# Block 1's causal mask on GpSimd, V projections from fp16 halves, another order of stages

## The chip, the cores and the metric

One Trainium2 chip, one core of it. The metric is device time in microseconds (us) of one execution. The kernel before took 839.89 us, the median of 3 runs (839.71 to 840.85).

## The reference, cut to what matters

The input x is (8, 256, 256): 8 batches of 256 tokens with 256 channels. Two blocks follow one another, each a residual sum over one LayerNorm:

```python
xn = _layernorm(x)
x = x + attn0(xn) + ffn0(xn)      # block 0
xn = _layernorm(x)
x = x + attn1(xn) + ffn1(xn)      # block 1
```

- attn0 and attn1 have 16 heads of 16 channels and a causal mask. attn0 adds ALiBi slopes, and clamps the probabilities from below at 1e-10, so a masked entry still counts. attn1 is a plain causal softmax: a masked entry is zero.
- ffn0 is a mixture of 8 experts (silu(x Wg) * (x Wu)) Wd, weighted per token by a router. ffn1 has ternary weights (256 to 1024 to 256) and a GELU between them; its output is quantized to 4 bits by a scale over the whole tensor, so no output can be written before the last batch's ffn1 is known.

## The kernel before, in words

Each batch is a set of tiles of 128 partitions; tokens are 2 tiles (NT), channels 2 (NK). The five engines each run their own list of steps, and the code of a step on an engine is a branch `if name == ...` in that engine's `do`. Orders are written out by hand in `FIRST_ORDER` (batch 0 of block 0, and the weights' preparation), `STEADY_ORDER` (a loop of 6 iterations: block 0 of batch n together with block 1 of batch n-1, and the beginning of batch n+1, marked +), `LAST_ORDER` and `FINAL_ORDER`. A number is a head of attention 0 (score, norm, turn, value steps at lags 0, 1, 3, 4). TensorE and the DMA queue of SyncE take this order as it is; ScalarE and VectorE shift steps by the offsets in `LAG`; GpSimd takes it as it is. Instructions of one engine are executed in order, and semaphores make them wait for other engines.

Steps that matter here:
- **ln0a, ln0b, tr0** (ln1a, ln1b, tr1 for block 1): VectorE computes the statistics and normalizes in place; GpSimd adds the output bias into `xb` (L790) and takes the power for rstd (L792); TensorE transposes in fp32 (L1032). ScalarE copies the result twice, to `xt` in fp32 (L902) and to `xt_hi` in fp16 (L903), and VectorE subtracts to get `xt_lo` (L1314). `xe_hi` and `xe_lo` are GpSimd's copies for the experts.
- **q, k, gate, up, down, w1**: products of fp16 halves, three products (hi*hi, lo*hi, hi*lo), or two where the weight is exact. Weights were multiplied by `WSCALE` = 16 before they were split (step **split**: ScalarE hi, VectorE or GpSimd lo).
- **v0:0, v0:1, v1** (L1070): the V projection, in fp32 from `xt` and `wv_sb`; v0 has the router's 8 columns beside the 256.
- **b, mp, m**: row maxima of block 1's scores, brought to a row `max_row` by way of `pieces` (GpSimd) and a bf16 product.
- **s:0 to s:7** (two heads each, `turn_ps[0]` and `[1]`): transposed scores on TensorE, plus the negated maximum (L1174), plus the mask: a product of `ident_b` with `later_b`, which holds -1e30 over the diagonal (L1177). ScalarE takes the exponential of 128x384 into `et` (L990).
- **y:0 to y:3** (four heads each): products of `et` with V (L1202) and with `ones` (L1208), the sum of the exponentials; VectorE divides (L1494, L1496). Then **op1** (L1126), the output projection.
- **up** on GpSimd: the low half `h0_lo` (L820) of the hidden layer, which **down** needs.
- **setup:1** on GpSimd builds `bias0`, slopes times distance (L801) plus the mask in `bias1` (L804), for block 0's scores.

In the loop GpSimd does nothing else than `pieces`, `xb`, rstd, `xe`, `h0_lo` and the low halves of h1.

## Time and profile before

| | us |
|---|---|
| median of 3 runs | 839.89 |
| profiled execution | 839.0 |
| its span | 837.3 |
| TensorE (PE) busy | 695.7 (83%) |
| VectorE (DVE) busy | 578.1 (69%) |
| ScalarE (ACT) busy | 478.3 (57%) |
| GpSimd (POOL) busy | 228.6 (27%) |

The profile comes from one execution. Rows name engine, line of the kernel, instruction, output and inputs, and shape. TensorE's matmuls are pipelined: the distance from one start to the next is what one costs, and the duration shown is longer than that. A number in brackets is the time in which the engine was idle before the row, with the instruction that ended the wait.

### The profile page before, as it was taken

To read this page: it belongs to the slowest core of one execution; us is meant where nothing else is said; L and a number is where in the kernel's file an instruction comes from. 1 tells how busy PE (TensorE), PEld (TensorE's weight loads), DVE (VectorE), ACT (ScalarE), POOL (GpSimd) and SP (SyncE) were. 2 spreads that over 40 slices of the span, in tenths; PEclk is the share of its full clock that TensorE was granted. 3 is DMA by queue.
4 is the path that set the end of the run, shared out by engine and by line. 5 is a ranking of instruction groups with operands and counts; after the bars stand their busy time and mean duration, and the time that the engine had idled before them with its cause. 6 is when DMAs were issued, how large, how long until landed. Compare 5 with 4: busy or idle time off the path is not lost.

```text
span 837.3 us, 19783 instructions
## 1 busy us (share of the span) xinstructions
PE 695.7 (83%) x6519; PEld 502.6 (60%) x6519; DVE 578.1 (69%) x2197; ACT 478.3 (57%) x1237; POOL 228.6 (27%) x260
## 2 busy tenths in 40 slices
...
GB/s 199 243 107 114 1 51 64 89 15 27 114 0 101 13 101 29 94 10 57 83 14 87 13 100 26 97 4 32 107 0 101 13 100 14 101 2 14 118 203 71
DMA packets 49544, 57.10 MB, mean 68 GB/s; under 512 B 5056, under 2 KB 40000, under 8 KB 49472
## 3 DMA queue, kind: packets, MB, share of 16 engines
...
## 4 chain that ended last, share of the span: by engine, by line
PE 61%; DVE 14%; ACT 8%; issue 8%; DMA 5%; ACTq 1%; SPq 1%; POOL 1%; DVEq 1%; POOLq 0%
PE gen_ps L1084 15%; PE gen_ps L1095 8%; PE value_ps L1202 7%; PE gen_ps L1058 5%; PE gen_ps L1126 3%; PE gen_ps L1070 3%; DVE probs L1461 3%; PE gen_ps L1115 3%; PE value_ps L1208 3%; PE turn_ps L1177 2%; PE score_ps L1139 2%; ACT hid L950 2%; PE turn_ps L1168 2%; DMA gu_lo<-x_dram 1%; PE turn_ps L1149 1%
## 5 line engine op out<-in xcount | busy, mean ns | idle before, releaser
L962 ACT ACTIVATE probs<-probs,nmax 128x256 f32<-128x256 f32 (+1 forms) x256 | 113.4, 445 | 57.8 <-DVE nmax L1461 57.3
L820 POOL TENSOR_TENSOR h_lo<-hid,h_hi 128x512 f16<-128x512 f32 x64 | 76.6, 1197 | 204.8 <-ACT h_hi L943 204.8
L1084 PE MATMUL gen_ps<-xe_hi,gu_hi 128*128 128x256 f16 x512 | 103.3, 285 | 8.4 <-DVE gated L1407 4.3
L1461 DVE CUSTOM_DVE_ANT_0 probs<-score_ps,bias 128x256 f32<-128x256 f32 (+1 forms) x256 | 80.5, 352 | 35.4 <-PE score_ps L1141 24.6
L1084 PE MATMUL gen_ps<-xe_lo,gu_hi 128*128 128x256 f16 x512 | 102.2, 283 | 0.0
L1475 DVE CUSTOM_DVE_ANT_0 junk<-score_ps,bias 128x256 bf16<-128x256 f32 (+1 forms) x256 | 76.1, 354 | 37.3 <-PE score_ps L1141 33.3
L1084 PE MATMUL gen_ps<-xe_hi,gu_lo 128*128 128x256 f16 x512 | 101.8, 282 | 0.0
L990 ACT ACTIVATE et<-turn_ps 128x384 f32<-128x384 f32 x128 | 55.8, 488 | 69.0 <-PE turn_ps L1177 69.0
L1486 DVE TENSOR_SCALAR probs<-probs,rsum 128x256 f32<-128x256 f32 (+1 forms) x256 | 81.3, 360 | 4.6
L1139 PE MATMUL score_ps<-k_stack,q_stack 64*128 64x256 f16 x256 | 37.7, 291 | 46.0 <-DVE nmax L1461 36.2
L971 ACT ACTIVATE pt<-turn_ps 128x384 f32<-128x384 f32 x128 | 61.2, 480 | 23.4 <-PE turn_ps L1151 23.4
L1412 DVE SCALAR_TENSOR_TENSOR hid<-gated,gen_ps 128x512 f32<-128x512 f32 x64 | 43.8, 685 | 41.9 <-PE gen_ps L1084 39.7
L1423 DVE SCALAR_TENSOR_TENSOR acc<-gen_ps,w,acc 128x256 f32<-128x256 f32 x112 | 48.7, 476 | 23.5 <-PE gen_ps L1095 23.5
L1084 PEld LDWEIGHTS gen_ps<-xe_hi,gu_hi 128*128 128x128 f16 x512 | 49.4, 102 | 24.5 <-issue 17.7
L1139 PEld LDWEIGHTS score_ps<-k_stack,q_stack 64*128 64x128 f16 x256 | 12.4, 93 | 80.0 <-DVE nmax L1461 40.2
L939 ACT ACTIVATE tanh_sb<-gen_ps 128x512 f32<-128x512 f32 x64 | 37.9, 592 | 38.6 <-PE gen_ps L1084 38.2
L833 POOL TENSOR_TENSOR h_parts<-hid,h_parts 128x512 f16<-128x512 f32 x32 | 36.7, 1160 | 84.6 <-ACT h_parts L957 84.6
L1084 PEld LDWEIGHTS gen_ps<-xe_lo,gu_hi 128*128 128x128 f16 x512 | 52.1, 102 | 8.0
L943 ACT ACTIVATE h_hi<-hid 128x512 f16<-128x512 f32 x64 | 40.0, 625 | 29.2 <-DVE hid L1412 25.3
L1084 PEld LDWEIGHTS gen_ps<-xe_hi,gu_lo 128*128 128x128 f16 x512 | 51.8, 101 | 7.7
L1407 DVE SCALAR_TENSOR_TENSOR gated<-tanh_sb,gen_ps 128x512 f32<-128x512 f32 x64 | 43.8, 685 | 17.7 <-ACT tanh_sb L939 16.9
L1095 PE MATMUL gen_ps<-wd_hi,h_hi 128*128 128x256 f16 x256 | 49.8, 277 | 4.9 <-issue 4.6
...
## 6 DMA issues: line engine op xcount, KB each, us to landing
...
```

What stands on the lines that cost most here:

```text
L820: pool.tensor_tensor(h0_lo[:, e], hid0[:, e], h0_hi[:, e], ALU.subtract).then_inc(s_h0l, 1)
L962: last = act.activation(probs[:, k, lo:hi], probs[:, k, lo:hi], ACT.Exp, scale=-1.0, bias=nmax[:, k, j:j + 1], accum_out=esum[:, k, j:j + 1])
L971: act.activation(pt[:, slot:slot + 3].rearrange("p t q -> p (t q)"), turn_ps[s % 2][:, 0:3 * P], ACT.Copy).then_inc(s_ev[0], 1)
L990: act.activation(et[:, s % TURNED], turn_ps[hp][:, 0:3 * P], ACT.Exp).then_inc(s_ev[1], 1)
L1084: last = pe.matmul(g[:, S * f:S * f + S], w[:, st.arg, m, k, cols], xx[:, k, :], start=(i == 0), stop=(i == len(terms) - 1))
L1095: last = pe.matmul(g[:, D * t:D * t + D], h[:, st.arg % 2, f, P * t:P * t + P], w[:, st.arg, f, :], start=(i == 0), stop=(i == len(terms) ...
L1139: pe.matmul(score_ps[hp][:, 0:S], q[rows[hp], i, P:S], k[rows[hp], i, :], start=True, stop=True)
L1202: last = pe.matmul(value_ps[PAD * j:PAD * j + PAD, lo:S], v, seen, start=(t == 0 and r == 0), stop=(t == 1 and r == 1), skip_group_check=( ...
L1423: dve.scalar_tensor_tensor(acc[:, t], g[:, D * t:D * t + D], w8[:, t, e:e + 1], (xb[0] if st.place == 0 else acc)[:, t], ALU.mult, ALU.add)\
L1461: last = dve.tensor_tensor_reduce(out=probs[:, k, lo:hi], in0=g[:, lo:hi], in1=bias0[:, s, blo:S], scale=-1.0, scalar=BIG, op0=ALU.add, op ...
L1475: last = dve.tensor_tensor_reduce(out=junk[:, hp, lo:hi], in0=score_ps[hp][:, lo:hi], in1=bias1[:, blo:S], scale=-1.0, scalar=BIG, op0=ALU ...
L1486: last = dve.tensor_scalar(probs[:, k, lo:hi], probs[:, k, lo:hi], rsum[:, k, j:j + 1], CLAMP, ALU.mult, ALU.max)
```

## The change

- The mask of block 1 goes from TensorE to GpSimd: the matmuls on `later_b` are gone; after each exponential an `affine_select` on GpSimd puts 0 into the entries above the diagonal of `et`; y waits for it (new semaphore `s_mk`).
- V is computed from fp16 halves of x and of Wv with the scale of 16, three products instead of one in fp32. `xt` and its copy are gone. A step `vsplit` splits Wv. The scale is taken out by `ones` = 16 in block 1, by the copy of `at[0]` in block 0, by `half_t` for the router; the bias is multiplied by 16.
- The mask in `bias0` becomes a selection instead of an addition.
- In the first batch LayerNorm writes to `acc` instead of over `x0`, so that it does not wait for the additions of the bias, which come behind the start of the weight loads.
- The four orders and the offsets of ScalarE and VectorE are others, and GpSimd has offsets too.

```diff
...
+       "gpsimd": {"s": 1, "up": 1, "s:6": -2, "last.b:1": 3, "v0:1": 1, "b:4": 4, "last.up": 2,
...
-    setup:0 ln0a split:1 xe split:0 ln0b split:3 tr0 setup:2 split:2 v0:0 q0 l0 k0 setup:1 split:5 rt1 gate:0 v0:1
...
+    ln0a setup:0 ln0b split:0 split:3 tr0 setup:2 xe split:2 vsplit:0 split:1 v0:0 q0 k0 gate:0 setup:1 l0 split:5 rt1
+    v0:1 split:4 up:0 gate:1 0 rt2 split:7 1 up:1 split:6 down:0 2 gate:2 3 down:1 4 up:2 split:8 gate:3 5 split:9
...
-    0 ln1a 1 ln1b gate:0 up:0 rt1 2 tr1 3 rt2 q1 k1 4 down:0 5 gate:1 6 up:1 7 gate:2 v1 w1:3 w1:0 w1:1 w1:2 l1 8 h1:0
-    up:2 9 10 h1:1 down:1 11 h1:2 gate:3 b:1 h1:3 up:3 down:2 12 13 14 15 b:0 16 gate:4 b:3 17 mp:0 up:4 b:4 18 down:3
-    b:2 +ln0a mp:1 w2 b:5 m:0 19 s:1 gate:5 op0 +ln0b s:0 b:6 +tr0 gate:6 up:5 down:4 s:2 +q0 b:7 y:0 s:3 +k0 up:6 +l0
-    +xe y:1 m:1 down:5 s:4 gate:7 +v0:0 s:5 up:7 s:6 y:2 s:7 down:7 y:3 +v0:1 down:6 op1
+    0 1 ln1a gate:0 2 ln1b up:0 rt1 tr1 3 rt2 4 q1 k1 5 gate:1 down:0 6 up:1 gate:2 w1:3 w1:0 l1 w1:2 w1:1 v1 7 8 h1:0
+    up:2 9 gate:3 10 h1:1 down:1 11 h1:2 b:1 h1:3 up:3 12 down:2 13 14 down:3 15 b:0 16 gate:4 17 b:3 mp:0 up:4 +ln0a
+    mp:1 18 b:2 w2 b:4 19 m:0 gate:5 s:1 b:5 down:4 +ln0b op0 s:0 b:6 +tr0 up:5 b:7 s:2 gate:6 +q0 +k0 s:3 y:0 +l0
+    up:6 m:1 gate:7 s:4 y:1 s:5 up:7 down:5 s:6 y:2 s:7 +v0:0 down:6 y:3 down:7 +v0:1 op1 +xe
...
-        wv_sb = [sb("wv0_sb", [P, NK, D + E]), sb("wv1_sb", [P, NK, D])]
+        wv_hi = [sb("wv0_hi", [P, NK, D + E], F16), sb("wv1_hi", [P, NK, D], F16)]
+        wv_lo = [sb("wv0_lo", [P, NK, D + E], F16), sb("wv1_lo", [P, NK, D], F16)]
...
-        later_b = sb("later_b", [P, NT, P], BF16)
...
-        xt = sb("xt", [P, NK, S])
...
+        et_flat = et[:].rearrange("p s q -> p (s q)")
+        wv_raw = [et_flat[:, 0:NK * (D + E)], et_flat[:, NK * (D + E):NK * (2 * D + E)]]
...
+                if n.reg is None and n.off == 1:
+                    sp.wait_ge(s_xb[0], NT)
...
-                pool.memset(ones[:, C:2 * C], 1.0).then_inc(s_tab, 1)
+                pool.memset(ones[:, C:2 * C], WSCALE).then_inc(s_tab, 1)
-                pool.affine_select(out=later_b[:], in_=later_b[:], compare_op=ALU.is_ge, fill=MASKED, base=0,
-                                   pattern=[[0, NT], [1, P]], channel_multiplier=-1).then_inc(s_tab, 1)
...
-                    if st.kind == "first":
-                        pool.wait_ge(s_ob, 32)
...
-                    for t in range(NT):
-                        pool.tensor_tensor(total[:, t], src[:, t], ob[l][:], ALU.add).then_inc(s_xb[l], 1)
+                    def add_bias():
+                        for t in range(NT):
+                            pool.tensor_tensor(total[:, t], src[:, t], ob[l][:], ALU.add).then_inc(s_xb[l], 1)
+
+                    early = st.kind == "first" and n.off == 0
+                    if not early:
+                        add_bias()
                     wait(pool, s_st[l], n.at(5, 5))
                     pool.tensor_tensor(rstd[l][:], var[l][:], minus_half[:], ALU.pow).then_inc(s_rstd[l], 1)
-                    if st.kind == "first" and n.off == 0:
+                    if early:
                         load_weights()
+                        pool.wait_ge(s_ob, 32)
+                        add_bias()
...
-                        pool.tensor_tensor(bias0[:, four], bias0[:, four], bias1[:].unsqueeze(1).broadcast_to(shape), ALU.add)\
-                            .then_inc(s_bias, 1)
+                        pool.affine_select(out=bias0[:, four, P:S], in_=bias0[:, four, P:S], compare_op=ALU.is_ge, fill=MASKED,
+                                           base=0, pattern=[[0, 4], [-1, P]], channel_multiplier=1).then_inc(s_bias, 1)
...
+                if name == "s":
+                    for hp in range(2):
+                        s = 2 * st.arg + hp
+                        wait(pool, s_ev[1], ahead(n).at(H, s + 1))
+                        if st.kind == "steady":
+                            settle(pool, s_gps)
+                        on_diagonal = et[:, s % TURNED, 0:2 * P].rearrange("p (t q) -> p t q", t=NT)
+
+                        pool.affine_select(out=on_diagonal, in_=on_diagonal, compare_op=ALU.is_ge, fill=0.0, base=0,
+                                           pattern=[[0, NT], [1, P]], channel_multiplier=-1).then_inc(s_mk, 1)
...
-            run_passes(pool, do, before_block1, {})
+            run_passes(pool, do, before_block1, LAG["gpsimd"])
...
+            for l, w in enumerate((wv0, wv1)):
+                act.dma_start(wv_raw[l].rearrange("p (k n) -> p k n", k=NK),
+                              w.rearrange("(k p) n -> p k n", p=P)).then_inc(s_wv[l], 16)
...
+                if name == "vsplit":
+                    act.wait_ge(s_wv[st.arg], 16)
+                    act.activation(wv_hi[st.arg][:].rearrange("p k n -> p (k n)"), wv_raw[st.arg], ACT.Copy, scale=WSCALE)\
+                       .then_inc(s_vhi, 1)
...
-                    act.activation(xt[:].rearrange("p k s -> p (k s)"), g[:, :], ACT.Copy).then_inc(s_xh[l], 1)
...
-                    act.activation(at[0][:, g], value_ps[:, 0:S], ACT.Copy).then_inc(s_at[0], 1)
+                    act.activation(at[0][:, g], value_ps[:, 0:S], ACT.Copy, scale=1.0 / WSCALE).then_inc(s_at[0], 1)
...
-                    src = (x0, acc)[l]
+                    src = acc if first else (x0, acc)[l]
...
-                        pe.wait_ge(s_wv0, 16)
+                        pe.wait_ge(s_vlo, 1)
...
-                        for k in range(NK):
-                            last = pe.matmul(o, xt[:, k, P * t:P * t + P], wv_sb[l][:, k, :],
-                                             start=(k == 0), stop=(k == NK - 1))
+                        terms = [(xx, w, k) for xx, w in ((xt_hi, wv_hi), (xt_lo, wv_hi), (xt_hi, wv_lo)) for k in range(NK)]
+                        for i, (xx, w, k) in enumerate(terms):
+                            last = pe.matmul(o, xx[:, k, P * t:P * t + P], w[l][:, k, :],
+                                             start=(i == 0), stop=(i == len(terms) - 1))
...
-                        pe.matmul(turn_ps[hp][:, 0:3 * P], pick[rows[hp], i, :], max_row[rows[hp], :], start=False, stop=False,
-                                  skip_group_check=True)
-                    for hp in range(2):
-                        pe.matmul(turn_ps[hp][:, 0:2 * P], ident_b[:], later_b[:].rearrange("p t q -> p (t q)"),
-                                  start=False, stop=True, skip_group_check=True).then_inc(s_tn[1], 1)
+                        pe.matmul(turn_ps[hp][:, 0:3 * P], pick[rows[hp], i, :], max_row[rows[hp], :], start=False, stop=True,
+                                  skip_group_check=True).then_inc(s_tn[1], 1)
...
-                    wait(pe, s_ev[l], m.at(H, G4 * (b + 1)))
+                    wait(pe, *(s_ev[0], m.at(H, G4 * (b + 1))) if l == 0 else (s_mk, m.at(H, G4 * (b + 1))))
...
-                    dve.tensor_scalar(half_t[:], half_t[:], 0.5, None, ALU.mult).then_inc(s_set, 1)
+                    dve.tensor_scalar(half_t[:], half_t[:], 0.5 / WSCALE, None, ALU.mult).then_inc(s_set, 1)
...
+                    for l in range(2):
+                        dve.tensor_scalar(vb[l][:], vb[l][:], WSCALE, None, ALU.mult).then_inc(s_set, 1)
+                if name == "vsplit":
+                    dve.wait_ge(s_vhi, st.arg + 1)
+                    dve.scalar_tensor_tensor(wv_lo[st.arg][:].rearrange("p k n -> p (k n)"), wv_raw[st.arg], WSCALE,
+                                             wv_hi[st.arg][:].rearrange("p k n -> p (k n)"), ALU.mult, ALU.subtract).then_inc(s_vlo, 1)
...
+                    early = n.reg is None and n.off == 0 and l == 0
+                    dst = acc if early else src
                     wait(dve, s_rstd[l], n.at(1, 1))
-                    wait(dve, s_xb[l], n.at(NT, NT))
+                    if not early:
+                        wait(dve, s_xb[l], n.at(NT, NT))
                     for t in range(NT):
-                        dve.tensor_scalar(src[:, t], src[:, t], mv[l][:, t, 0:1], rstd[l][:, t:t + 1],
+                        dve.tensor_scalar(dst[:, t], src[:, t], mv[l][:, t, 0:1], rstd[l][:, t:t + 1],
...
+                    if l == 0 and st.arg == 0 and n.reg is None and n.off == 0:
+                        dve.wait_ge(s_set, SET_VB)
```

## Rows read from the trace of the kernel before

**Rows 1.** Windows: stretch, length; busy us of PE, PEld, DVE, ACT, POOL; PEclk, DMA share.
```profile
0.00:131.50 131.50, 72.65 (x518) 52.16 (x518) 87.58 (x227) 68.35 (x149) 75.39 (x80) 0.88 0.38 120
...
131.50:695.20 563.70, 507.33 (x4884) 371.04 (x4885) 398.37 (x1606) 334.61 (x900) 118.44 (x143) 0.95 0.17 54
```

**Rows 2.** TensorE in order of time: start us, duration us, instruction, idle before.
```profile
160.43 0.28 PE L1139 MATMUL score_ps<-k_stack,q_stack 64*128 64x256 f16 x2 [1.01 <-DVE nmax L1461]
...
327.90 0.39 PE L1058 MATMUL gen_ps<-xt_hi,qk_hi 128*128 128x256 f16 x2 [2.45 <-DVE xt_lo L1314]
348.75 0.28 PE L1139 MATMUL score_ps<-k_stack,q_stack 64*128 64x256 f16 x2 [1.01 <-DVE nmax L1461]
...
361.07 0.28 PE L1139 MATMUL score_ps<-k_stack,q_stack 64*128 64x256 f16 x2 [2.08 <-DVE nmax L1461]
...
538.06 0.28 PE L1139 MATMUL score_ps<-k_stack,q_stack 64*128 64x256 f16 x2 [1.01 <-DVE nmax L1461]
```

**Rows 3.** Windows of 10 us within iterations, columns as in rows 1.
```profile
359.20:369.20 10.00, 7.86 (x79) 5.57 (x80) 9.36 (x53) 6.74 (x24) 0.91 (x1) 1.00 0.01 2
...
379.20:389.20 10.00, 10.00 (x119) 7.32 (x114) 5.95 (x23) 5.59 (x12) 0.55 (x3) 1.00 0.01 2
...
409.80:419.80 10.00, 5.33 (x40) 3.87 (x39) 6.91 (x32) 3.98 (x12) 2.11 (x3) 0.76 0.17 55
```

**Rows 4.** TensorE in order of time: v1, an s step's mask, v0.
```profile
339.97 1.89 PE L1070 MATMUL gen_ps<-wv_sb,xt 128*128 128x256 f32 x8
341.70 0.38 PE L1106 MATMUL gen_ps<-xt_hi,t_sb 128*128 128x256 f16 x2
341.92 0.38 PE L1106 MATMUL gen_ps<-xt_lo,t_sb 128*128 128x256 f16 x2
...
398.07 0.39 PE L1177 MATMUL turn_ps<-later_b,ident_b 128*128 128x256 bf16 x2
398.30 0.38 PE L1084 MATMUL gen_ps<-xe_hi,gu_hi 128*128 128x256 f16 x2
...
405.40 1.16 PE L1070 MATMUL gen_ps<-wv_sb,xt 128*128 128x264 f32 x4
...
406.39 0.38 PE L1095 MATMUL gen_ps<-wd_hi,h_hi 128*128 128x256 f16 x2
```

**Rows 5.** Groups of ScalarE instructions: busy us, mean ns, idle before.
```profile
L990 ACT ACTIVATE et<-turn_ps 128x384 f32<-128x384 f32 x128 | 55.8, 488 | 69.0 <-PE turn_ps L1177 69.0
...
L902 ACT ACTIVATE xt<-gen_ps 128x512 f32<-128x512 f32 x16 | 9.5, 596 | 12.2 <-PE gen_ps L1032 11.6
```

**Rows 6.** Groups of GpSimd instructions.
```profile
L820 POOL TENSOR_TENSOR h_lo<-hid,h_hi 128x512 f16<-128x512 f32 x64 | 76.6, 1197 | 204.8 <-ACT h_hi L943 204.8
...
L790 POOL TENSOR_TENSOR xb<-acc,ob_sb 128x256 f32<-128x256 f32 x16 | 11.3, 726 | 56.6 <-DVE yx_sb L1449 46.1 <-DVE acc L1430 7.7 <-DVE acc L1423 2.8
...
L804 POOL TENSOR_TENSOR bias<-bias 128x1024 f32<-128x1024 f32 x4 | 10.2, 2559 | 0.3
...
L760 POOL TENSOR_SCALAR_AFFINE_SELECT pick<-pick 128x512 bf16<-128x512 bf16 x4 | 3.4, 846 | 0.4
...
L754 POOL TENSOR_SCALAR_AFFINE_SELECT later_b<-later_b 128x256 bf16<-128x256 bf16 x1 | 0.4, 415 | 0.0
```

**Rows 7.** All engines in order of time, in the first batch.
```profile
8.57 1.40 POOL L790 TENSOR_TENSOR xb<-x,ob_sb 128x256 f32<-128x256 f32 x2 [5.35 <-DMA ob_sb<-in_ob]
...
18.46 1.06 ACT L893 ACTIVATE wd_hi<-v_sb 128x1024 f16<-128x1024 f32 x1 [5.84 <-DMA v_sb<-in_wd]
...
21.52 2.10 PE L1070 MATMUL gen_ps<-wv_sb,xt 128*128 128x264 f32 x4 [5.55 <-DVE xt_lo L1314]
...
41.13 0.59 PE L1084 MATMUL gen_ps<-xe_hi,gu_hi 128*128 128x256 f16 x2 [4.34 <-DVE gated L1407]
```

**Rows 8.** One line of VectorE: duration ns min/median/max, first and last start.
```profile
L1345 DVE SCALAR_TENSOR_TENSOR r_zone<-r_in,r_zone x8: 174/176/2306, 38.0 to 699.5; 128x16 f32<-128x16 f32 x8
```

**Rows 9.** A group of VectorE instructions.
```profile
L1407 DVE SCALAR_TENSOR_TENSOR gated<-tanh_sb,gen_ps 128x512 f32<-128x512 f32 x64 | 43.8, 685 | 17.7 <-ACT tanh_sb L939 16.9
```

More of the change, by code:

```diff
@@ L73 @@
 TURNED = 6
-LAG = {"scalar": {"score": 4, "up": 4, "q0": 1, "turn": -1, "value:1": 6, "s": 1, "score:1": 4,
[18 rows of a table removed]
-           "turn": -3, "last.score": -2, "final.quant": 3, "steady.gate:4": 2, "final.mp:0": 2,
[5 rows of a table removed]
+LAG = {"scalar": {"score": 4, "up": 5, "q0": 1, "value:1": 5, "s": 1, "score:1": 4, "steady.down:2": -3,
[41 rows of a table added]
 def in_turn(items, key):
@@ L139 @@
 FIRST_ORDER = """
-    setup:0 ln0a split:1 xe split:0 ln0b split:3 tr0 setup:2 split:2 v0:0 q0 l0 k0 setup:1 split:5 rt1 gate:0 v0:1
-    split:4 up:0 gate:1 rt2 split:7 split:6 down:0 up:1 0 1 gate:2 2 down:1 3 up:2 split:8 gate:3 4 5 split:9 up:3
-    down:2 tern:0 split:10 6 tmx:0 tern:1 split:11 gate:4 7 down:3 8 9 up:4 10 11 12 tern:2 gate:5 down:4 tern:3 13
-    split:13 +ln0a split:12 up:5 tern:4 tsm:0 tern:5 gate:6 14 up:6 gate:7 +ln0b 15 tern:6 up:7 16 down:5 tmx:1 tern:7
-    17 +tr0 18 tern:8 down:6 +q0 +k0 tern:9 +v0:0 19 +v0:1 +xe +l0 tsm:1 tern:10 tern:11 down:7 op0
+    ln0a setup:0 ln0b split:0 split:3 tr0 setup:2 xe split:2 vsplit:0 split:1 v0:0 q0 k0 gate:0 setup:1 l0 split:5 rt1
@@ L145 @@
+    v0:1 split:4 up:0 gate:1 0 rt2 split:7 1 up:1 split:6 down:0 2 gate:2 3 down:1 4 up:2 split:8 gate:3 5 split:9
+    up:3 down:2 tern:0 split:10 6 tmx:0 tern:1 gate:4 7 down:3 8 split:11 9 up:4 10 11 12 gate:5 tern:3 down:4 13
+    tern:2 split:13 +ln0a tern:4 up:5 tsm:0 tern:6 split:12 tern:5 gate:6 14 gate:7 +ln0b up:6 down:5 15 16 tmx:1 up:7
+    vsplit:1 +tr0 17 down:6 tern:8 tern:7 +q0 +k0 tern:9 +v0:0 +l0 18 19 +v0:1 down:7 op0 +xe tsm:1 tern:10 tern:11
 """
 STEADY_ORDER = """
-    0 ln1a 1 ln1b gate:0 up:0 rt1 2 tr1 3 rt2 q1 k1 4 down:0 5 gate:1 6 up:1 7 gate:2 v1 w1:3 w1:0 w1:1 w1:2 l1 8 h1:0
@@ L151 @@
+    mp:1 18 b:2 w2 b:4 19 m:0 gate:5 s:1 b:5 down:4 +ln0b op0 s:0 b:6 +tr0 up:5 b:7 s:2 gate:6 +q0 +k0 s:3 y:0 +l0
+    up:6 m:1 gate:7 s:4 y:1 s:5 up:7 down:5 s:6 y:2 s:7 +v0:0 down:6 y:3 down:7 +v0:1 op1 +xe
 """
 LAST_ORDER = """
-    ln1a gate:0 rt1 0 ln1b rt2 1 tr1 2 gate:1 up:0 3 q1 k1 4 down:0 5 up:1 6 gate:2 v1 w1:1 w1:2 w1:0 w1:3 l1 7 up:2 8
-    h1:1 down:1 9 gate:3 10 11 12 h1:0 h1:3 13 b:0 up:3 14 down:2 15 h1:2 b:1 gate:4 16 up:4 b:4 gate:5 17 18 b:3
-    down:3 19 b:2 mp:0 up:5 down:4 b:5 gate:6 up:6 b:7 m:0 gate:7 s:2 b:6 down:5 mp:1 up:7 s:0 down:6 op0 down:7 s:1
```

34 lines of the change are left out of this document (20 added, 14 removed), and 63 rows, old and new, of the table LAG.

## The prediction

> **What bounds the kernel now.** I read the busy time by stretch first. The profiled execution took 839.0 us, with a span of 837.3 us; the median of the runs shown is 839.89 us, 0.9 us more. The first batch takes 131.5 us, of which TensorE is busy for 72.7; the 563.7 us of the loop's six iterations hold 507.3 us of TensorE [rows 1]. So TensorE is nearly full in the loop, and in the first batch nothing is: there the chain of weight loads, splits and router decides.
>
> Then TensorE's timeline, where a number in brackets is the idle time before the row. The same wait (1.01 us) stands at 160.43 and 538.06 with four iterations between them, which makes an iteration 377.63 / 4 = 94.4 us [rows 2]. The idle stretches lie in its first half: 2.45 us between tr1 and q1 (ScalarE copies the transposed block twice, VectorE subtracts), 1.01 and 2.08 us before score matmuls that wait for VectorE [rows 2].
>
> Third, ten-us windows. In 359-369 TensorE is busy for 7.86 us and VectorE for 9.36; in 379-389 TensorE for 10.00 and VectorE for 5.95 [rows 3]. The second half of an iteration, where the steps s, y, v0 and the next batch's q0 and k0 stand, is bound by TensorE, instruction for instruction; the first half is a chain through VectorE, ScalarE and TensorE. After the loop's boundary TensorE waits, and its granted clock was 0.76 there [rows 3], between the levels 1.2 and 2.4 GHz: some of this stretch ran at the lower. I take no gain from that, but a shorter idle stretch could give some back.
>
> **The change, part by part.** *The mask on TensorE goes.* Every s step ended with a pair of bf16 matmuls on ident_b and later_b: from 398.07 to the next row at 398.30, 0.23 us for the pair [rows 4]. There are 8 per batch, 64 in all. They stand where TensorE has no gap, so all of it counts: -64 x 0.223 = -14.3 us, with 0.218 to 0.23 for a pair. The bounds are -8 (if s waits for ScalarE to empty turn_ps as often as TensorE is held by its own work) and -17 (part of them at the lower clock).
>
> *V from halves.* The eight fp32 matmuls of v1 took from 339.97 to 341.70, 1.73 us or 216 ns each; an fp16 pair of the same 256 columns took 341.92 - 341.70 = 0.22 us, 109 ns each [rows 4]. Now there are 24 of these: 2.61 us, +0.88 per batch. A v0 step had four fp32 matmuls of 264 columns, 405.40 to 406.39, 0.99 us [rows 4]; twelve fp16 ones of 264 columns take about 12 x 110 = 1.32 us, +0.33, twice per batch. v0 stands in the bound half: 16 x 0.33 = +5.3 us. v1 stands in the half with gaps; I let half of its 8 x 0.88 = 7.0 us be swallowed: +3.5. Sum +8.8, between +5.3 and +12.3. The split itself costs more TensorE time than fp32; it is paid by the mask.
>
> The Trainium skill, page "FP8 and Floating Point Precision", section "TensorE Precision Notes", says that true fp32 makes four passes through the array. By that, three fp16 products would be a saving of a quarter, and v1 would fall from 32 to 24 passes. The rows here have fp32 at 216 / 109 = two fp16 matmuls; by the page's four, each of the 64 + 64 fp32 matmuls would save one of 109 ns, -14 us instead of +8.8. The measurement decides.
>
> *One copy less on ScalarE.* The copy into xt (L902) took 596 ns on average, 16 times [rows 5]. It stands between tr1 and q1, where TensorE waits in every iteration; overlap of neighbouring ScalarE instructions leaves about 0.5 us. Eight of tr1: -4; as one of these waits is short I take -3.5. The eight of tr0 stand in the half where TensorE has other work: 0.
>
> *The selection on GpSimd.* It reads and writes 128x256 fp32 with one input. Nearest rows: a one-input selection over 128x256 bf16, 415 ns (L754); over 128x512, 846 ns (L760); above these a two-input addition over 128x256 fp32, 726 ns (L790) [rows 6]. I take 0.42 us, with 0.3 to 0.73 as bounds: 16 per batch, 6.7 us, on an engine that is busy for 118 of 564 us in the loop [rows 1], so capacity is no question; latency is. Between s:7 and y:3 TensorE now has v0:0 (1.32) and down:6 (1.31), 2.6 us; the way is two exponentials on ScalarE (488 ns each, [rows 5]) and the last selection, 1.4 to 1.9 us. For y:2, up:7 (the same size as down:6), down:5 and s:6 cover. So 0 in the loop. In the final pass nothing covers the last y: +0.4 us and as much for a quant addition in its way, +0.8 (0 to +3). What queues behind a selection on GpSimd is h_lo of the up steps (1197 ns each, [rows 6]), which down needs two steps later.
>
> *The first batch.* Its additions of ob waited for their load until 8.57 us, and only then came rstd. Now LayerNorm goes on at once and writes into acc. But the first row of TensorE that mattered was 21.52 us, v0:0 behind the copies and xt_lo, which stood behind split:2, whose weights landed at 18.46 [rows 7]. By the new order v0:0 still stands first on TensorE and waits for vsplit:0 on VectorE, which stands behind split:2 (one ScalarE copy and one VectorE subtraction, some 2.3 us): about 21.5 us again. The early LayerNorm is hidden by that load. What comes after is better: gate:0 no longer stands behind v_sb in VectorE's queue behind l0's subtraction, worth about 2.5 us, and the four bias additions of 2.56 us (L804) become one-input selections over 512 columns (846 ns), 4 x 1.7 = 6.9 us less of GpSimd, while TensorE waited 4.34 us for a gated of VectorE at 41.13 [rows 7]. The longer v0:0 costs 0.7. The load of batch 1's x now waits for the additions too, but it has some 70 us of time. I take -3 (bounds +4, if the orders around the weight splits are worse, and -10).
>
> *The order.* In the steady pass gate:3 moves ahead of score:10 and down:2 between score:12 and score:14. These are the places of the 1.01 and 2.08 us waits, and each step is 1.31 us of TensorE: 2.3 us could be filled. VectorE is 94% busy there, so I count half, -1.16. Against it, on VectorE ln1b now stands behind gate:0 (685 ns, [rows 9]) and score:2 (about as much: 1.4 us later), of which score:4 and turn:1 ahead of q1 fill 0.65: +0.75. Net -0.4 per iteration; seven such passes: -2.9 (bounds -16 and +10).
>
> **Sum.** -14.3 + 8.8 - 3.5 + 0.8 - 3 - 2.9 = -14.1. 839.0 - 14.1 = 824.9; with the 0.9 us between profile and median, 825.8 us.
>
> **Rivals.** *A, the first half has the last word in the order too.* The moved steps fill the whole 2.3 us, the l1 step ahead of v1 brings the stack loads earlier, and the clock rises earlier behind shorter gaps: another 1.5 to 2.5 us per pass, 7 x 2 = -14, so 812 us. For it: those waits recur in each iteration. Against: VectorE's 9.36 us in ten [rows 3].
>
> *B, the wait of y on GpSimd takes the place of the mask.* GpSimd is in order; if h_lo of up:7 (1.2 us) comes ahead of the selections of s:7, and those of s:5 are late, the path becomes 1.0 + 1.2 + 0.8 = 3.0 us against 2.6 of cover, and y:3 and op1 slip; op1 is the last step of an iteration and VectorE's next LayerNorm hangs on it. At 1.6 us for y:3 and 1.2 for y:2, 8 x 2.8 = +22: 848 us, slower. It decides from a selection that takes 1 us or more, or from h_hi of up:7 later than s:6's exponentials. Against: the rows have 415 ns.
>
> *C, VectorE held by GpSimd.* In the first batch a 128x16 VectorE instruction (L1345) took 2306 ns against a median of 176, just while a bias addition of 2.6 us ran on GpSimd [rows 6, 8]. If each selection held a VectorE instruction of the chain for its own 0.42 us half of the time, it would be 8 x 16 x 0.21 = +27 us on VectorE; as VectorE has 4 of 10 us free beside the s steps, a third lands, +9: 835 us. The Trainium skill, page "SBUF — State Buffer", section "SBUF: two separate sides", speaks against this change: a GpSimd instruction and a VectorE instruction with two SBUF inputs or in a two-port mode exclude each other for their whole length. The 2306 ns agree with it; but in the s stretch most VectorE work reads PSUM, and there l0's subtraction is the only long one with two SBUF inputs.
>
> *D, gains and costs cancel*: the s steps are in truth paced by ScalarE's two exponentials and v1 is not swallowed: -8 + 12.3 - 3.5 + 0.8 - 1 - 0 = +0.6: 840 us.
>
> **Chances.** Forecast 0.5 (own range 819 to 832), A 0.24, C 0.1, D 0.06, B 0.1. What a measurement can tell from no change is about 0.2%, 838.2 to 841.6 us. D is mostly within that; B is slower, and of C, whose price could double, a fifth is. Faster 0.8, within 0.2% 0.06, slower 0.14. The range from 809 to 840 leaves out B, a part of D and the end of A.
>
> **What would show it.** An iteration of about 93.2 us (the same score wait four iterations apart); 0.88 us more in v1 and 0.33 more in each v0, with 109 ns per fp16 matmul; no L1177; tr1 to q1 shorter by 0.5; a selection of 0.42 us; y without idle time ahead of it except in the last 20 us; a first batch of 128 us. I am wrong in the mechanism if TensorE waits for GpSimd in the loop (B), if VectorE's means rise (C), and in a size if the waits before the score matmuls vanish or grow by more than a us.

## The result, and the profile after

The changed kernel takes 794.78 us (median; 790.95 to 795.63), the kernel before beside it 839.93: ratio 0.945, interval 0.9423 to 0.9477. It is faster. The time is 31 us below the forecast of 825.8 and below the range of 809 to 840. The profiled execution took 790.95 us.

Windows of the changed kernel, columns as in [rows 1]; the borders are the first and the seventh start of block 1's transposes (tr1), so that six whole iterations lie between them:

```profile
0.00:127.68 127.68, 71.05 (x559) 51.85 (x559) 90.86 (x255) 71.38 (x161) 70.31 (x79) 0.88 0.41 127
127.68:655.26 527.58, 478.88 (x4820) 355.75 (x4820) 391.67 (x1607) 321.44 (x884) 152.12 (x240) 0.97 0.18 58
655.26:789.20 133.94, 104.35 (x1077) 73.76 (x1077) 86.37 (x341) 72.95 (x179) 45.41 (x67) 0.91 0.25 80
```

The same six iterations of the kernel before:

```profile
136.45:700.46 564.01, 504.40 (x4872) 369.12 (x4869) 399.11 (x1608) 333.07 (x894) 119.34 (x144) 0.95 0.16 53
```

So of the 48.1 us between the two spans (837.3 and 789.2), 36.4 are the loop's, 8.8 lie ahead of the first tr1 and 2.9 in the tail (133.9 against 136.8). In the loop an iteration falls from 94.0 to 87.9 us. TensorE's busy time falls by 25.5 us and its idle time by 10.9 (59.6 to 48.7), and the clock granted to it rises from 0.95 to 0.97.

TensorE of the changed kernel at one boundary of iterations, in order of time:

```profile
297.06 0.29 PE L1180 MATMUL score_ps<-k_stack,q_stack 64*128 64x256 f16 x2 [1.69 <-issue]
...
299.83 0.28 PE L1180 MATMUL score_ps<-k_stack,q_stack 64*128 64x256 f16 x2 [1.01 <-DVE nmax L1511]
...
304.35 1.12 PE L1072 MATMUL gen_ps<-ident,acc 128*128 128x128 f32 x4 [2.77 <-DVE acc L1357]
...
306.92 0.39 PE L1180 MATMUL score_ps<-k_stack,q_stack 64*128 64x256 f16 x2 [0.80 <-DVE nmax L1511]
...
308.04 0.63 PE L1098 MATMUL gen_ps<-xt_hi,qk_hi 128*128 128x256 f16 x2
308.47 0.63 PE L1098 MATMUL gen_ps<-xt_lo,qk_hi 128*128 128x256 f16 x2
```

These answer to [rows 2]. The 2.45 us between tr1 and q1 are gone (no idle time stands at 308.04). Of the 1.01 and 2.08 us in mid iteration one wait of 0.53 us is left. In their place tr1 now waits 2.77 us for ln1b, where the same boundary had 0.30 before. That boundary is the mildest of the old kernel: over the six that end an iteration of the loop the wait at tr1 was 1.17 us on average and is 2.79. Behind this boundary the rows of TensorE stand 0.43 us apart (at 308.04) and from 311 on 0.22 us: the lower and the higher of the two clock levels.

The V projections (v1, then the step v0:0), which answer to [rows 4], and the selection, with the columns of [rows 6]:

```profile
322.50 0.39 PE L1111 MATMUL gen_ps<-wv_hi,xt_hi 128*128 128x256 f16 x2
...
323.82 0.27 PE L1190 MATMUL turn_ps<-ident,probs 128*128 128x128 f32 x1
...
375.86 0.40 PE L1111 MATMUL gen_ps<-wv_hi,xt_hi 128*128 128x264 f16 x2
...
376.55 0.38 PE L1136 MATMUL gen_ps<-wd_hi,h_hi 128*128 128x256 f16 x2
```
```profile
L853 POOL TENSOR_SCALAR_AFFINE_SELECT et<-et 128x256 f32<-128x256 f32 x128 | 49.9, 416 | 25.9 <-ACT et L1029 25.9
```

v1 takes 1.32 us where it took 1.73, v0 0.69 where it took 0.99: shorter, not longer. A selection is 0.416 us, as forecast.

### The profile page after: what moved, and what is told of

The parts are those of the page before. It is cut to its first block and busy times, and to the rows that moved or that the text cites. A ratio compares the mean times of both kernels' runs of the same rounds, so it can differ in the third digit from the quotient of the medians.

```text
span 789.2 us, 19922 instructions
## 1 busy us (share of the span) xinstructions
PE 654.3 (83%) x6455; PEld 481.4 (61%) x6455; DVE 568.9 (72%) x2201; ACT 465.8 (59%) x1223; POOL 267.8 (34%) x386
## 5 line engine op out<-in xcount | busy, mean ns | idle before, releaser
L844 POOL TENSOR_TENSOR h_lo<-hid,h_hi 128x512 f16<-128x512 f32 x64 | 74.2, 1160 | 203.5 <-ACT h_hi L982 203.3
L1125 PE MATMUL gen_ps<-xe_hi,gu_hi 128*128 128x256 f16 x512 | 101.6, 281 | 3.2 <-DVE gated L1457 2.0
L1536 DVE TENSOR_SCALAR probs<-probs,rsum 128x256 f32<-128x256 f32 (+1 forms) x256 | 74.6, 334 | 4.5
L1473 DVE SCALAR_TENSOR_TENSOR acc<-gen_ps,w,acc 128x256 f32<-128x256 f32 x112 | 48.8, 477 | 25.5 <-PE gen_ps L1136 25.4
L853 POOL TENSOR_SCALAR_AFFINE_SELECT et<-et 128x256 f32<-128x256 f32 x128 | 49.9, 416 | 25.9 <-ACT et L1029 25.9
L1125 PEld LDWEIGHTS gen_ps<-xe_hi,gu_hi 128*128 128x128 f16 x512 | 46.1, 100 | 18.7 <-issue 11.8
L982 ACT ACTIVATE h_hi<-hid 128x512 f16<-128x512 f32 x64 | 40.2, 629 | 18.3 <-DVE hid L1462 17.1
```

Source lines behind the costliest of these rows:

```text
L844: pool.tensor_tensor(h0_lo[:, e], hid0[:, e], h0_hi[:, e], ALU.subtract).then_inc(s_h0l, 1)
L853: pool.affine_select(out=on_diagonal, in_=on_diagonal, compare_op=ALU.is_ge, fill=0.0, base=0, pattern=[[0, NT], [1, P]], channel_multipli ...
L1125: last = pe.matmul(g[:, S * f:S * f + S], w[:, st.arg, m, k, cols], xx[:, k, :], start=(i == 0), stop=(i == len(terms) - 1))
L1473: dve.scalar_tensor_tensor(acc[:, t], g[:, D * t:D * t + D], w8[:, t, e:e + 1], (xb[0] if st.place == 0 else acc)[:, t], ALU.mult, ALU.add)\
L1536: last = dve.tensor_scalar(probs[:, k, lo:hi], probs[:, k, lo:hi], rsum[:, k, j:j + 1], CLAMP, ALU.mult, ALU.max)
```

## The experiments

Kernels that ran together share their runs of the kernel before. Its median was between 839.3 and 843.1 us from round to round, and the ratios' intervals are 0.3 to 0.9% to either side; so the times alone don't tell a difference of less than some 4 us between two programs of different rounds, and the traces have to. Each part was first made alone in the kernel before, then undone alone in the changed one.

**One part alone.** v_alone:

```diff
-  4 matmuls (2 in v0): pe.matmul(o, xt[:, k, ...], wv_sb[l][:, k, :], ...)
+  12 matmuls (6): for xx, w in ((xt_hi, wv_hi), (xt_lo, wv_hi), (xt_hi, wv_lo))
```

> The kernel before with V from fp16 halves (vsplit steps put into its own order, one ScalarE copy less), nothing else. Theory: one fp32 matmul of 256 columns is two records of 216 ns, so it costs four fp16 matmuls and not two; then 64 fp32 matmuls save about 0.11 us each, -7 to -9 us, and the copy 3 to 5 us more: 827 to 830 us. Rival (the prediction's reading, two fp16 matmuls for one fp32): +8.8 - 3.5, about 845 us. In the trace v1 takes 1.31 us by the theory and 2.61 us by the rival.

837.29 us against 841.36, ratio 0.9955 (0.9919 to 0.9992). V from halves, with the copy gone, makes the old kernel faster, by less than the theory's 827 to 830 us; an iteration takes 93.0 us where it took 94.0, and TensorE's busy time in six of them falls from 504.4 to 499.2 us.

mask_alone: the matmuls on later_b out, the selections in, in the old order.

```diff
-  pe.matmul(turn_ps[hp][:, 0:2 * P], ident_b[:], later_b[:]...)
+  pool.affine_select(out=on_diagonal, in_=on_diagonal, compare_op=ALU.is_ge, fill=0.0, ...)
```

> The kernel before with block 1's mask as a selection on GpSimd, in the old order of stages and with no offsets on GpSimd. Theory: the matmuls save 14 us, but on GpSimd the old order has xe, which waits for up:7, ahead of the selections of s:4 and s:5, so y:2 waits some 2.7 us per iteration and much of the 14 us is lost: 835 to 846 us, with TensorE waiting for GpSimd at y. Rival: the selection is hidden in any order, 826 us.

893.51 us, ratio 1.0643 (1.055 to 1.0737): 52 us slower, far beyond both theories. GpSimd and TensorE of it in one iteration, in order of time:

```profile
402.04 0.19 POOL L842 CAST pieces<-nmax 128x16 bf16<-128x16 f32 x1 [13.42 <-DVE nmax L1505]
402.31 0.22 POOL L844 TENSOR_TENSOR pieces<-nmax,pieces 128x16 bf16<-128x16 f32 x1
402.49 1.49 POOL L834 TENSOR_SCALAR_AFFINE_SELECT et<-et 128x256 f32<-128x256 f32 x4
...
417.26 0.40 POOL L820 COPY xe_hi<-xt_hi 128x256 int32<-128x256 int32 x1 [5.64 <-DVE hid L1442]
...
417.95 1.48 POOL L834 TENSOR_SCALAR_AFFINE_SELECT et<-et 128x256 f32<-128x256 f32 x4
```
```profile
404.08 0.86 PE L1220 MATMUL value_ps<-et,v_sb 128*32 128x256 f32 x16 [3.71 <-issue]
...
419.49 1.51 PE L1220 MATMUL value_ps<-et,v_sb 128*32 128x256 f32 x16 [2.69 <-POOL et L834]
```

Four selections run in one go as soon as a step ahead of them in GpSimd's queue is let go: mp:1's pieces, which wait for VectorE's maxima of b:7 (13.42 us idle), and xe, which waits for VectorE (5.64 us). The exponentials of the two groups of four were done 8 and 2 us before. The profile puts 22.4 us of y's waits down to these selections (sum, number, longest):

```profile
PE value_ps L1220 <- POOL et L834: 22.4, 10, 4.1
```

That leaves out rows such as the one at 404.08, whose 3.71 us have no releaser named though they end where the four selections end. Both rows come back in every iteration of the loop, 3.7 and 2.69 us, and make up 6.4 of the 7.7 us by which an iteration grew (94.0 to 101.7).

mask_moved is the same kernel with these two steps put behind the selections:

```diff
-  run_passes(pool, do, before_block1, {})
+  run_passes(pool, do, before_block1, {"steady.mp:1": 12, "steady.xe:0": 20})
```

> mask_alone (old orders, mask on GpSimd) with two steps of the loop moved behind the selections on GpSimd alone: mp:1 behind s:1 and xe behind down:7. Theory: the 52 us that mask_alone lost came from GpSimd's queue, where selections stood behind xe and pieces, which wait for VectorE; with these moved the 14 us of matmuls are won in the loop: 826 to 832 us. Rival: the selection itself, or its latency in y, costs the 52 us; then 870 us or more.

840.55 us, ratio 0.9974 (0.9936 to 1.0012), between the two theories. Two steps of GpSimd moved win 53 us back, but the 14 us or more that the mask frees on TensorE don't show in the time. Its trace says where they went. In six iterations TensorE is busy 17.5 us less than before (486.9) and the loop is 9.5 us shorter (554.5 against 564.0); y still waits 1.03 us per iteration for the selections. Outside the loop the two steps were not moved: the first tr1 comes 3.1 us later, and the stretch from the seventh on is 7.7 us longer (144.5), with waits of y for the selections of 4.36 and 1.43 us in it.

order_alone (the four orders and all offsets, and the load of Wv in two parts, which mask_alone has too) and first_alone (LayerNorm into acc, the late bias, the selection in bias0):

```diff
-  STEADY_ORDER = """ 0 ln1a 1 ln1b gate:0 up:0 rt1 2 tr1 3 ...
+  STEADY_ORDER = """ 0 1 ln1a gate:0 2 ln1b up:0 rt1 tr1 3 ...
```
```diff
-  src = (x0, acc)[l]
+  src = acc if first else (x0, acc)[l]
```

> The kernel before with the new orders and offsets alone (no vsplit, mask on TensorE, V in fp32, first batch as before). Theory: the order is the larger part of what the prediction missed, 15 to 20 us: 820 to 825 us, most of it in the loop's iterations. Rival 1 (the prediction): 3 us, 837 us. Rival 2: the order is only good together with the mask on GpSimd, 838 us or more.

> The kernel before with the first batch's LayerNorm into acc, the additions of the bias behind the weight loads, and the selection in bias0, in the old order. Theory: v0 stays behind split:2, so the early LayerNorm is hidden; only GpSimd's shorter bias work counts: 836 to 839 us. Rival: the first batch's whole 11 us comes from here, 829 us.

order_alone takes 816.81 us, ratio 0.9726 (0.9633 to 0.9818); first_alone 842.98, 1.003 (0.9992 to 1.0069). The order is more than half of the gain; the first batch's edits show none.

**One part undone** in the changed kernel (the diffs above, the other way round):

> The changed kernel with V in fp32 again, with the copy into xt and without the vsplit steps. Theory: fp32 costs four fp16 matmuls, so v1 goes from 1.31 to 1.73 us and each v0 step from 0.66 to 0.99, 1.08 us per batch, 8.7 in all, and the copy delays q1 by 0.5 us per batch: 9 to 13 us slower than the changed kernel. Rival: V alone on the old order gave only 4 us, so the gap is 4 us or less here too.

> The changed kernel with block 1's mask on TensorE again, as 64 pairs of bf16 matmuls of 0.22 us, and no selections in et. Theory: 14 us slower than the changed kernel, all of it TensorE busy time, since TensorE has no gap beside the s steps. Rival: part of the selection's latency was paid at y, so that only 5 to 10 us are lost.

> The changed kernel with the first batch's LayerNorm over x0, behind the additions of the bias, and the mask added into bias0. Theory: v0 waits for wv_lo behind split:2 anyway, so 0 to 2 us slower; the first tr1 stood at 128.8 us in order_alone and at 127.7 in the changed kernel. Rival: 5 to 9 us slower, since the first batch became 9 us shorter.

undo_v 795.45 us (ratio to the kernel before 0.9436, 0.9393 to 0.9479), undo_mask 814.80 (0.9646, 0.9597 to 0.9694), undo_first 794.59 (0.9425, 0.9382 to 0.9468). By the medians the mask is worth 20.0 us in the new order, V 0.7 and the first batch's edits nothing; the last two can't be told from zero, and both theories of undo_v fell. By the ratios the mask is worth 0.0196 of the time, 16.5 us, give or take 5, so the times alone don't exclude 14.3. The trace does decide: an iteration of undo_mask takes 90.95 us, 3.0 more than the 87.93 of the changed kernel, 18 us in six.

Why is the mask worth more than 64 x 0.223 = 14.3? TensorE of undo_mask, in order of time, then of the changed kernel at the same steps:

```profile
364.89 0.33 PE L1208 MATMUL turn_ps<-max_row,pick 64*128 64x384 bf16 x2
365.14 0.39 PE L1211 MATMUL turn_ps<-later_b,ident_b 128*128 128x256 bf16 x2
365.47 0.28 PE L1173 MATMUL score_ps<-k_stack,q_stack 64*128 64x256 f16 x2
...
368.24 0.39 PE L1211 MATMUL turn_ps<-later_b,ident_b 128*128 128x256 bf16 x2
368.46 0.38 PE L1118 MATMUL gen_ps<-xe_hi,gu_hi 128*128 128x256 f16 x2
```
```profile
356.44 0.33 PE L1215 MATMUL turn_ps<-max_row,pick 64*128 64x384 bf16 x2
356.60 0.27 PE L1180 MATMUL score_ps<-k_stack,q_stack 64*128 64x256 f16 x2
...
359.10 0.33 PE L1215 MATMUL turn_ps<-max_row,pick 64*128 64x384 bf16 x2
359.36 0.39 PE L1125 MATMUL gen_ps<-xe_hi,gu_hi 128*128 128x256 f16 x2
```

With the mask it is 0.58 us from the pick row to the score (364.89 to 365.47), without it 0.16, so there the mask costs 0.42. Ahead of a gate step it costs only the 0.22 us that the forecast read (the pick row is 0.25 or 0.26 us from a mask and from a gate step alike). Ahead of y's value matmuls it costs 0.33, as one more pair of rows shows, of undo_mask (without the mask pick to value takes 0.25, 363.57 to 363.82):

```profile
372.92 0.39 PE L1211 MATMUL turn_ps<-later_b,ident_b 128*128 128x256 bf16 x2
373.25 0.42 PE L1236 MATMUL value_ps<-et,v_sb 128*32 128x256 f32 x4
```

In these rows some 0.1 us more stands wherever the part of TensorE's array that a row names (64\*128, 128\*128, 128\*32) changes with the next row. The pick row ahead of a score keeps its 64\*128 and has no such extra, though columns and type change; nor has the mask pair ahead of a gate step, both 128\*128. That this alone does it was not tried. From the first row of an s step to the next step the eight s steps of an iteration add up to 5.75 us in undo_mask and 3.25 in the changed kernel: 0.31 us for a pair (two at 0.42, three at 0.33, three at 0.22), and 64 x 0.31 = 20.

Why V is worth nothing there, though it takes 8 x 0.41 + 16 x 0.30 = 8.1 us off TensorE: ten us from tr1, of the changed kernel and of undo_v (windows, columns as in [rows 3]):

```profile
304.35:314.35 10.00, 9.19 (x60) 7.25 (x61) 8.95 (x49) 6.74 (x21) 1.16 (x1) 0.68 0.01 2
```
```profile
305.32:315.32 10.00, 7.81 (x70) 6.36 (x71) 9.40 (x52) 8.23 (x25) 1.16 (x1) 1.00 0.01 2
```

In undo_v the granted clock of the ten us from tr1 is 1.00 at four of the six boundaries and 0.66 at the other two, and iterations that begin with the one take 88 us, with the other 90. In the changed kernel it is below 1.00 at all six (0.66 to 0.83, 0.68 here), and an iteration takes 88.3 to 88.8. The last iteration before the seventh tr1 is shorter in both, 84.4 and 85.2. The mean is 88.1 and 87.9. So the TensorE work that is saved meets a lower clock and more idle time at the boundary. That the one causes the other was not tried.

**What in the order.** steady_only (the loop's order and its offsets alone, in the kernel before) and two_moves:

```diff
-  up:2 9 10 h1:1 down:1 11 h1:2 gate:3 b:1 h1:3 up:3 down:2 12 13 14
+  up:2 9 gate:3 10 h1:1 down:1 11 h1:2 b:1 h1:3 up:3 12 down:2 13 14
```

> The kernel before with one part of the change: the loop's order of stages (STEADY_ORDER) and, for the looped iterations alone, the new offsets of the engines. The first batch, the last two iterations, the mask, the V projections and the tile of the transposes stay as they were. The whole order alone took 23 us off (816.8), of which the six looped periods between the transposes held 3.5 us each (94.0 to 90.5) = 21 and the first batch 7.6, the tail gave 4 back. Theory 1 (the loop's order is worth its 3.5 us per iteration whatever stands around it): 839.9 - 21 = 819, range 815 to 824, period 90.5. Rival (the periods shorten only because the first batch's order leaves the engines in another phase): 830 or more, period above 93.

> The kernel before with two stages moved in STEADY_ORDER and nothing else: gate:3 ahead of score:10, down:2 between score:12 and score:13. They are put where TensorE stood 1.01 and 2.08 us behind the scores, where the granted clock fell a second time in each iteration. Theory 1 (the second fall of the clock is most of what the loop's order gained): the second fall is gone and the period of 94.0 us falls by 1.5 to 3.5 us, 821 to 831 us. Rival (VectorE's maxima end there late whatever TensorE does, and the gain of the order lies in the boundary): within 3 us of before, 837 to 843, the wait only shows up some scores further on.

steady_only takes 820.99 us against 839.27 (ratio 0.9766, 0.973 to 0.9802), an iteration 90.4 us: as expected, the loop's order works by itself. two_moves takes 834.86 (0.9913, 0.988 to 0.9946), a quarter of that, and between what its two theories gave. TensorE of it, where the 2.08 us stood:

```profile
453.36 0.28 PE L1153 MATMUL score_ps<-k_stack,q_stack 64*128 64x256 f16 x2 [1.35 <-DVE nmax L1487]
454.80 0.47 PE L1163 MATMUL turn_ps<-ident,probs 128*128 128x128 f32 x1 [0.62 <-DVE probs L1512]
```

The 2.08 us have become 1.35 and 0.62: down:2 fills little, as VectorE sets the pace and the scores wait again two steps on.

old_offsets and old_vector (the changed kernel with the offsets of ScalarE and VectorE, and of VectorE alone, as before):

```diff
-  "vector": {"gate": 1, "up": -1, "down": 2, "op0": 2, "w2": 2, "l1": 1, ...
+  "vector": {"gate": 1, "up": -1, "down": 2, "op0": 2, "w2": 2, "l1": 2, ...
```

> The changed kernel with the offsets of ScalarE's and VectorE's own orders as in the kernel before; TensorE's order of stages is the new one. Theory 1 (TensorE's order carries the gain, the offsets follow): 794 to 799 us. Rival (the offsets carry the order's gain, since VectorE is what TensorE waits for behind the scores): 808 or more, with VectorE's releases of scores later than in the changed kernel.

> The changed kernel with VectorE's offsets as in the kernel before; ScalarE's and GpSimd's and TensorE's order are the new ones. With both engines' offsets old the time was 823.6 us, 29 above the changed kernel. Theory 1 (the waits for nmax and for acc, both VectorE's, grew in that run, so VectorE's offsets carry it): 815 to 826. Rival (ScalarE's exponentials, hid and et, stand too late by its old offsets, and VectorE follows): 794 to 803.

823.64 us (0.9801, 0.9763 to 0.9838) and 810.40 (0.9674, 0.9627 to 0.9721). Theory 1 of old_offsets fell; in old_vector less was lost than its theory's 815 to 826 us. With TensorE's new order and the old offsets 29 us are lost, 16 of them by VectorE's; the other 13 are a difference, as ScalarE's offsets alone were not tried. TensorE of old_vector at the boundary:

```profile
306.53 0.28 PE L1176 MATMUL score_ps<-k_stack,q_stack 64*128 64x256 f16 x2 [1.51 <-DVE nmax L1507]
311.05 0.66 PE L1068 MATMUL gen_ps<-ident,acc 128*128 128x128 f32 x4 [2.77 <-DVE acc L1353]
314.12 0.40 PE L1176 MATMUL score_ps<-k_stack,q_stack 64*128 64x256 f16 x2 [2.09 <-DVE nmax L1507]
```

The wait at tr1 is the same 2.77 us, the score waits around it are 0.5 and 1.3 us longer.

gpsimd_plain (GpSimd's own offsets taken away):

```diff
-  run_passes(pool, do, before_block1, LAG["gpsimd"])
+  run_passes(pool, do, before_block1, {})
```

> The changed kernel with GpSimd's own offsets taken away: its steps stand where TensorE's order puts them. Moving the cast pieces away from the selections in the kernel before won back 53 us, so the place of GpSimd's steps can decide. Theory 1 (here the new order alone keeps the selections clear of the casts, the offsets move only b:5, y and m:1 by a step or two): 794 to 800. Rival (the offsets are what keeps them clear, and TensorE waits for s_mk at y): 803 or more, with waits at y behind POOL above 2.1 us in all.

797.27 us (0.9515, 0.9472 to 0.9558); y waits 3.3 us for POOL in all, against 2.1. 2.5 us, no more than theory 1 allowed: by the new order alone mp:1 stands ahead of all selections and xe behind them.

keep_copy puts the ScalarE copy back:

```diff
+  act.activation(xt[:].rearrange("p k s -> p (k s)"), g[:, :], ACT.Copy).then_inc(s_xh[l], 1)
   act.activation(xt_hi[:].rearrange("p k s -> p (k s)"), g[:, :], ACT.Copy).then_inc(s_xh[l], 1)
-  wait(dve, s_xh[l], n.at(1, 1))
+  wait(dve, s_xh[l], n.at(2, 2))
```

> The changed kernel with ScalarE's fp32 copy of the transposed block put back into a tile of its own, ahead of the fp16 copy; VectorE waits for both, nothing reads it. It is 17 copies of about 0.45 us. Theory 1 (TensorE works at scores and turns meanwhile and waited only 0.4 us in all for the halves, so the copy was hidden in this order): 793 to 797. Rival (the prediction's term, the copy stands on the chain from the transposes to q and k): 3.5 us more, 797 to 800.

794.19 us (0.9488, 0.9432 to 0.9543). The interval is too wide to tell 0 from 3.5 us; the trace does: six iterations take 526.5 us with the copy and 527.6 without. The copy was hidden: theory 1.

**Can the wait at tr1 be used?** Three edits of the changed kernel:

```diff
 ln1b_early, VectorE's offsets:
+  "steady.ln1b:0": -3
 gate1_fill, STEADY_ORDER; gate1_late the same, with offsets 4 and 9 for gate:1 on ScalarE and VectorE:
-  up:0 rt1 tr1 3 rt2 4 q1 k1 5 gate:1 down:0 6
+  up:0 gate:1 rt1 tr1 3 rt2 4 q1 k1 5 down:0 6
```

> The changed kernel with one edit: in the looped iterations VectorE normalizes the input of block 1 (ln1b) directly behind gate:0, ahead of score:2's subtraction and gate instead of behind it. In each iteration TensorE stands 2.77 us for that normalization before block 1's transposes, and its clock falls behind. Theory 1 (that wait sets the boundary and the clock's fall): the wait shortens by about 0.7 us, 6 x 0.7 = 4 us off, 790, and down to 780 if the clock's fall goes with it. Rival (score:2's release is then later by as much, and TensorE waits there): 793 to 797, no difference. If the subtraction of score:2 was on the path: slower by 2 to 5 us.

> The changed kernel with one step of STEADY_ORDER moved: gate:1 (1.31 us of TensorE) from behind score:5 to directly ahead of rt1 and tr1, where TensorE stands 2.77 us for VectorE's normalization in each iteration. Theory 1 (that time is free on TensorE and nothing waits for gate:1's tanh and gating, 0.7 us of VectorE, ahead of score:3's): up to 1.3 us per iteration, seven such passes, -9, and a little of the clock: 783 to 790. Rival (VectorE is the chain here, 9 us of 10 busy, and its gating of gate:1 moved ahead of score:3 delays the scores by as much): 793 to 800, the wait moves to score:3 and score:4.

> The same move of gate:1 on TensorE, but ScalarE's tanh and VectorE's gating of it stand about where they stood (behind up:0 and behind norm:3), so that nothing is put ahead of the normalizations. If gate1_fill fails by VectorE's 0.7 us alone: 783 to 790 here. Rival (its gen_ps buffer is held that long, and q1 or k1 waits for one): 795 or more.

ln1b_early takes 800.67 us (0.952, 0.9481 to 0.9558), gate1_fill 798.34 (0.9499, 0.9456 to 0.9542), gate1_late 818.04 (0.9721, 0.9682 to 0.9761); the changed kernel was at 0.945. TensorE at the boundary, in this order of the kernels:

```profile
308.77 0.66 PE L1072 MATMUL gen_ps<-ident,acc 128*128 128x128 f32 x4 [1.55 <-DVE acc L1357]
312.48 0.39 PE L1180 MATMUL score_ps<-k_stack,q_stack 64*128 64x256 f16 x2 [2.73 <-DVE nmax L1511]
```
```profile
309.17 0.65 PE L1072 MATMUL gen_ps<-ident,acc 128*128 128x128 f32 x4 [1.53 <-DVE acc L1357]
313.38 0.39 PE L1180 MATMUL score_ps<-k_stack,q_stack 64*128 64x256 f16 x2 [3.23 <-DVE nmax L1511]
```
```profile
319.35 0.28 PE L1180 MATMUL score_ps<-k_stack,q_stack 64*128 64x256 f16 x2 [1.50 <-DVE nmax L1511]
326.22 0.61 PE L1098 MATMUL gen_ps<-xt_hi,qk_hi 128*128 128x256 f16 x2 [4.74 <-DVE gated L1457]
```

In the first two 1.2 us go from tr1's wait at this boundary, as meant (at three others of ln1b_early only 0.4), and 1.9 and 2.4 us come to the next score's (0.80 in the changed kernel here, 1.6 at other boundaries). An iteration grows from 87.9 to 88.5 and 88.4 us. In the third gate:1 holds its gen_ps buffer until VectorE takes it behind norm:3, and q1 waits 4.74 us for it. So the rivals of the two gate:1 runs held, and ln1b_early came out slower, as its third reading had it. VectorE is busy for 8.8 to 9.0 of the ten us from tr1 in the changed kernel, and filling TensorE there buys nothing. No version beats the changed kernel by more than 0.1% (undo_first and keep_copy are level with it).

## Why the prediction was wrong

Four steps of the prediction failed, in this order of size: *The order*, which it took at -0.4 us per iteration and a part of the first batch's -3, and which gave 3.5 us per iteration and 24.6 in all; *V from halves*, whose +8.8 had the wrong sign; the -14.3 of the mask, too small, where -16.5 to -20.0 was measured against its bound of -17; and the -3.5 of the copy, which gave nothing. In the table its terms stand beside what the runs gave, in us, from the medians, each with some 4 us of doubt (order_alone 8).

| step | forecast | measured |
|---|---|---|
| mask off TensorE, selection in | -14.3 + 0.8 | -20.0 (undo_mask; -16.5 by the ratios) |
| V from halves | +8.8 | -0.7 with the copy (undo_v), -4.1 with it in the old kernel (v_alone) |
| one ScalarE copy less | -3.5 | 0 (keep_copy: 794.2 with it) |
| first batch's edits | part of -3 | 0 (undo_first) |
| order, first batch's and loop's | -2.9 and the rest of -3 | -24.6 (order_alone), of it -18.3 the loop's (steady_only) |
| sum | -14.1 | -45.2 |

*V from halves* had the wrong sign. The step that failed is "The eight fp32 matmuls of v1 took from 339.97 to 341.70, 1.73 us or 216 ns each". The code has four (two tiles of rows by two of k); the trace of [rows 4] shows x8, as it has two records for each fp32 matmul; a v0 step has two, and x4. One takes 1.73 / 4 = 0.43 us, four times the 109 ns of an fp16 one, and three fp16 products are cheaper: 12 x 0.110 = 1.32 us, as measured. The prediction cited the Trainium skill, page "FP8 and Floating Point Precision", section "TensorE Precision Notes", with its four passes for fp32, and set it aside for a count of records that the code would have corrected. The page was right: by it and the true count, the estimate is 64 matmuls less one pass of 0.109, -7 us, against the 8.1 in the trace.

*The mask* was right in mechanism, TensorE's time beside the s steps, and too small in size: the pair was read ahead of a gate step (0.22 us), where it is cheapest; the mean is 0.31. That this time comes out as gain needed the new order: in the old one mask_moved shows none of it in the total.

*The order* is the largest miss. The prediction priced it by the waits that the moved TensorE steps could fill and took half of that (-1.16 per iteration), less 0.75 for ln1b. two_moves shows that this reading was fair for those two steps: -4.4 us, 0.9 per iteration in the trace (94.0 to 93.1). What it missed is the rest: the iteration of order_alone is 90.5 us, 3.5 less, with TensorE idle for 47.4 us of six iterations instead of 59.6 and 8.9 us less busy for the same work, with the clock at 0.98 instead of 0.95. The failed step is that pricing: it took the order of TensorE's steps for the whole. The offsets of ScalarE and VectorE, of which the prediction counted only ln1b, cost 29 us when they are taken back (old_offsets), more than the 24.6 of the whole order. Some 33 entries for the loop changed on each of the two engines; which of them matter stays open. Idle time at ln1b was foreseen at +0.75 per iteration and came at +1.6 in the changed kernel (2.79 against 1.17 on average), yet the waits behind it, 1.7 to 2.5 us at q1, vanished.

*The first batch.* The programs with the old first order start tr1 at 133.8 to 140.7 us (mean of seven profiles 138.5), those with the new one at 126.9 to 131.5 (mean of twelve 129.6); 9 us, and 3 were forecast. The reason given was right in part: TensorE's row of v0:0 is at 21.30 us where it was at 21.52, and LayerNorm ends early for nothing (9.39 us, then this wait):

```profile
21.30 0.62 PE L1111 MATMUL gen_ps<-wv_hi,xt_hi 128*128 128x264 f16 x2 [10.83 <-DVE wv_lo L1291]
```

The gain comes later: of the waits in [rows 7] the 4.34 us for gate:0's gating at 41.13 are 1.99 us at 31.39, ten us earlier. In order_alone, without vsplit, v0:0 starts at 15.14 us, and yet its first tr1 stands at 128.8 us against 127.7: the six us at v0:0 don't reach the loop. The chain that sets the first tr1 was not traced.

*The copy* was hidden, with score:4 and turn:1 between tr1 and q1; the prediction used that cover for ln1b (0.65 us) and counted the copy in full as well.

*Rivals.* A (812 us) came nearest, still 17 us too slow; its moved steps were not the reason, as two_moves shows. B, y behind GpSimd, is real: 6.4 us of waits per iteration and 52 us of time in mask_alone; there the condition was not the selection's length or h_lo, as the prediction had it, but GpSimd steps that wait for VectorE ahead of it. In the changed kernel y waited 2.1 us for the selections, in three waits behind 730 us and none in the loop. C fell, as far as means can tell: with the selections and, in undo_mask, without them VectorE's two kinds of maxima take 352 and 352 ns against 352 and 353, the multiplication by rsum 334 against 334. D fell with V's sign.
